# Retention's second half: output projection in three passes of rounded parts and remainders, one batch later; ScalarE takes the first ternary step

## The chip, the core and the metric

The kernel runs on one core of a Trainium2 chip. The metric is the device time of one execution in microseconds (us). TensorE (PE) multiplies, VectorE (DVE), ScalarE (ACT) and GpSimd (POOL) work on rows, and SyncE (SP) issues most DMAs. Each engine runs its own instructions in order and waits on semaphores.

## What is computed

The reference is two layers, each an attention-like block and a feed-forward block. The change lies in the first block, a retention, and in the preparation of weights for the next one:

```python
O = jnp.einsum('hst,bthe->bshe', A, V).reshape(b, s, dim)
mu = O.mean(axis=-1, keepdims=True)
var = O.var(axis=-1, keepdims=True)
Y = (O - mu) / jnp.sqrt(var + GN_EPS) * gn_gamma + gn_beta
W = jax.nn.relu(x @ wg_w)
return W * Y @ wo_w
...
def weight_quant(w):            # of w1, w3 and w2 of the feed-forward block
    scale = 1.0 / jnp.clip(jnp.mean(jnp.abs(w)), EPS)
    return jnp.clip(jnp.round(w * scale), -1.0, 1.0) / scale
```

There are 8 batches of 256 rows of 512 columns. A row block is 128 rows (a chunk), so a batch has two.

## The kernel before

`retention` has two halves. The first leaves V in `vt` (v_rows in the profile), the gate W transposed in `wt` (gate_t), and the summed scores in `at` (a_t). The second half, the one that changes, is one block of code in which the engines meet at a barrier before and after. For each batch b:

- PE: `turn` (L744) transposes the two chunks of normalised rows y; then `pv(b+1)` (L729, L732) makes the attention output of the next batch in `o_bank`; then the projection (L756) multiplies gated rows z_t by `wo` in fp32 into `p_bank`, 4 matmuls a chunk, each recorded as two.
- ACT: L776 scales and shifts the transposed rows from `y_bank` into z_t, four instructions a chunk.
- DVE: `gate` (L819) multiplies z_t by W; `normalise(b+1)` is bn_stats (L209) and its small followers (L212 to L216), POOL's power for the reciprocal root (L222), and L812, which writes y; `residual` (L823) adds `p_bank` to x.

Beside this runs the preparation of the feed-forward block. ACT sums |w3| and |w2| (`abs_sum`, L358). From batch 3 (QUIET) on, DVE turns half a weight a batch into ternary values in three steps over 2816 columns: `to_grid` (L371), `off_grid` (L377) and the cast into tern_w (L835), which counts up `tern_ready`. The first two tiles of the feed-forward's rows are normalised early too (`ffn.moments`, `ffn.normal` L288, `ffn.grid` L300, `ffn.integers` L307).

SP issues 28 DMA transposes in a fixed order, after the loads of wo and of two weights: 11 of w1 and 11 of w3 (L680), which write over v_rows that are no longer needed; two of quantised rows (L320); four of w2 (L683). `first_batch_past` is 3 for w1 and 6 for w3: so many batches' v_rows must be free. In the kernel before, a batch of v_rows is free once `pv` has read it, so SP waits for `o_ps`, the count of finished output chunks.

After the block, `bit_ffn` starts: its first matmuls (L968) need the barrier, which waits for all engines, SP among them, and the transposed rows and w1.

Of the kernel before, what the change touches and what calls it, by code (L numbers as in the profile page):

```python
# [336 lines left out]
def retention(nc, st, keep, sem, sbuf, psum, a, x, x_rows, ctx_rows, ident, powers, tern, w_mean, raw, vt, turned, kt_d, vc_d, upto):  # L337
# [311 lines left out]
    with ExitStack() as sb_:  # L649
        wo = sbuf(sb_, "wo", [P, KD, D])  # L650
        gam = sbuf(sb_, "gn_gamma", [P, KD])
        bet = sbuf(sb_, "gn_beta", [P, KD])
        y = sbuf(sb_, "gn_y", [P, CB, D])
        zt = sbuf(sb_, "z_t", [P, CB, D])
# [8 lines left out]
        o_ps, y_ready, y_ps, y_scaled, z_ready, p_ps, x_added = (  # L663
            sem(n) for n in ("o_ps", "y_ready", "y_ps", "y_scaled", "z_ready", "p_ps", "x_added"))
# [5 lines left out]
        def _(sp):  # L670
# [25 lines left out]
            sp.wait_ge(o_ps, CB * B)  # L696
# [2173 lines left out]
```

## Time and profile before

| what | us |
|---|---|
| median of 3 runs (1151.67 to 1154.88) | 1152.2 |
| the profiled execution, its own time | 1151.06 |
| its span | 1149.2 |
| PE busy in the span | 1072.1 (93%) |
| second half of retention, first matmul to last residual | 133.75 to 241.34 |
| first matmul of the feed-forward block | 242.02 |

Times in the rows are counted from the start of the span. The span leaves out 1.9 us of the execution. The blocks follow each other with barriers, and PE is busy nearly throughout, so a block that ends later moves what follows.

### The profile page before, as it was taken

Reading aid. Unit: us, or ns where it says so; the run is one execution under the profiler, and the core shown is the slowest. Engines: PE = TensorE matmul, PEld = TensorE weight load, DVE = VectorE, ACT = ScalarE, POOL = GpSimd, SP = SyncE. Lnnn points to the kernel's source line nnn. Section 1 sums busy time; section 2 is a strip of 40 time slices with the busy share of each in tenths; the row PEclk is TensorE's granted clock in tenths of the full one; section 3 lists DMA queues with packets and bytes.
Section 4 is the critical chain, followed back from the end, with each engine's and each line's share of the span. In section 5 each row is a group of like instructions: output and inputs, shape, how many; then the busy total and the mean of one; then the engine's idle time right before and its main releaser. Section 6 shows DMA issues by size and latency. Waiting matters only on the chain. (4 is left out here: it accounts for less than half of the span.)

```text
span 1149.2 us, 21701 instructions
## 1 busy us (share of the span) xinstructions
PE 1072.1 (93%) x5899; PEld 813.8 (71%) x5912; DVE 836.3 (73%) x1579; ACT 475.3 (41%) x1011; POOL 444.5 (39%) x355
## 2 busy tenths in 40 slices
PE   7999799989996998999899987999999999999997
PEld 7989765634443577888887665777777777777773
DVE  4548457969998557778897985868688687766656
ACT  2232235246562378878322162333333333333320
POOL 0000012225541101766761002666666666556620
PEclk9999999999997998999898998999999999999998
DMA  8424350433334586573264314889899899787759
GB/s 304 156 92 173 133 182 10 85 66 66 62 65 81 195 300 230 177 255 121 73 233 165 83 37 153 227 203 257 188 254 254 201 259 256 194 200 185 140 120 366
DMA packets 148189, 195.49 MB, mean 170 GB/s; under 512 B 62985, under 2 KB 80777, under 8 KB 148144
## 3 DMA queue, kind: packets, MB, share of 16 engines
q1 hardware_dynamic: 130512, 156.61, 42.8%
q0 software_dynamic: 17632, 38.32, 16.8%
q8 instruction: 23, 0.38, 0.2%
q14 instruction: 22, 0.18, 0.1%
HBM read 136.56 MB, written 50.34 MB: 163 GB/s over the span
## 5 line engine op out<-in xcount | busy, mean ns | idle before, releaser
L2462 POOL DMA_INDIRECT y_d<-tail,x_ox x78 | 144.0, 1846 | 124.3 <-ACT tail L2689 107.7
L1738 POOL DMA_INDIRECT e_rows<-r_d,x_ix x80 | 103.3, 1291 | 115.4 <-issue 96.3
L2534 PE MATMUL x_h<-x_w_hi,x_t_hi 128*128 x320 | 127.9, 400 | 2.2 <-DVE x_t_lo L2703 2.2
L2535 PE MATMUL x_h<-x_w_lo,x_t_hi 128*128 x320 | 127.7, 399 | 0.0
L2536 PE MATMUL x_h<-x_w_hi,x_t_lo 128*128 x320 | 127.6, 399 | 0.0
L2703 DVE TENSOR_TENSOR x_w_lo<-w,x_w_hi (+1 forms) x64 | 112.5, 1759 | 9.8 <-ACT x_w_hi L2660 2.6
L2651 ACT ACTIVATE e_rows<-x_h 128x256 f32<-128x256 f32 x80 | 30.8, 385 | 184.1 <-PE x_h L2536 184.1
L222 POOL TENSOR_TENSOR ln_rstd<-ln_ve,powers 128x2 f32<-128x2 f32 (+1 forms) x40 | 35.1, 878 | 165.8 <-DVE ln_ve L216 165.8
L2703 DVE TENSOR_TENSOR x_t_lo<-x_xb,x_t_hi 128x512 fp32r<-128x512 f32 x80 | 55.2, 691 | 44.6 <-ACT x_t_hi L2646 43.3
L1615 DVE SCALAR_TENSOR_TENSOR raw<-h_qk,h_d 128x768 f32<-128x768 f32 x64 | 58.2, 950 | 25.4 <-PE h_qk L1494 9.2
L2553 PE MATMUL x_o<-x_w_hi,x_avt_hi 128*128 x160 | 74.0, 463 | 1.2 <-issue 0.7
L2534 PEld LDWEIGHTS x_h<-x_w_hi,x_t_hi 128*128 128x128 f32 x320 | 60.9, 190 | 17.5 <-issue 2.6
L2535 PEld LDWEIGHTS x_h<-x_w_lo,x_t_hi 128*128 128x128 f32 x320 | 60.9, 190 | 14.9
L2536 PEld LDWEIGHTS x_h<-x_w_hi,x_t_lo 128*128 128x128 f32 x320 | 60.8, 190 | 14.9
L1381 ACT ACTIVATE h_d<-h_negm,h_g 128x256 f32<-128x256 f32 x128 | 63.7, 497 | 6.3 <-DVE h_negm L1595 2.9
L756 PE MATMUL p_bank<-wo,z_t 128*128 128x512 f32 x128 | 58.3, 610 | 6.9 <-DVE z_t L819 6.9
L2750 DVE SCALAR_TENSOR_TENSOR e_rows<-e_rows,x_rw,x_h 128x256 f32<-128x256 f32 x80 | 38.2, 477 | 35.7 <-ACT e_rows L2651 34.8
L2554 PE MATMUL x_o<-x_w_lo,x_avt_hi 128*128 x160 | 63.2, 395 | 0.0
L627 PE MATMUL ring<-xt,wg 128*128 128x256 f32 x256 | 56.6, 379 | 0.0
L1508 PE MATMUL h_pv<-h_v,raw 128*128 128x99 f32 x256 | 55.3, 300 | 0.0
L2689 ACT COPY tail<-x_o 128x512 f32<-128x512 f32 x78 | 46.0, 589 | 18.2 <-PE x_o L2559 18.2
L1509 PE MATMUL h_pv<-h_v,raw 128*128 128x99 f32 x256 | 52.9, 291 | 0.0
(419 smaller groups left out, 2564.6 us busy)
## 6 DMA issues: line engine op xcount, KB each, us to landing
w<-in_L_ffn_w SPq DMA_DIRECT2D x32, 1024.0 KB, 9.2
w<-in_L_ffn_w SPq DMA_DIRECT2D x32, 512.0 KB, 8.3
h_negm<-negm_d SPq DMA_DIRECT2D x15, 1024.0 KB, 7.5
raw<-in_L_ffn_w SPq DMA_DIRECT2D x3, 2816.0 KB, 16.5
x_res<-in_x SPq DMA_DIRECT2D x8, 512.0 KB, 4.5
ctx_in<-in_ctx SPq DMA_DIRECT2D x8, 512.0 KB, 3.4
kt_d<-ct SPq DMA_DIRECT2D x8, 512.0 KB, 3.3
vc_d<-ctx_in SPq DMA_DIRECT2D x8, 512.0 KB, 2.6
```

Of the source, the lines that this page charges most:

```text
L627: last = nc.tensor.matmul(ring[3 + n][:, j * S:(j + 1) * S], wg[:, k, m * P:(m + 1) * P], xt[:, k, :], start=k == 0, stop=k == KD - 1)
L756: last = nc.tensor.matmul(p_bank[c][:], zt[:, c, k * P:(k + 1) * P], wo[:, k, :], start=k == 0, stop=k == KD - 1)
L1381: nc.scalar.activation(dm[:, k % 2, j, 0:2, :], nm[:, u, h, 0:2, :], ACT.Exp, bias=gst[:, u, 0, h:h + 1])
L1615: nc.vector.scalar_tensor_tensor(cm[:, k % 2, heads], qk[:, heads, 0:3 * P], float(DH) ** -0.5, dm[:, k % 2, heads].rearrange("p j c n -> ...
L1738: nc.gpsimd.indirect_dma_start(out=xg[q][s], out_offset=None, in_=r_d, in_offset=bass.IndirectOffsetOnAxis(ap=ix[q][:, s:s + 1], axis=0), ...
L2462: nc.gpsimd.indirect_dma_start(out=y_d[s], out_offset=bass.IndirectOffsetOnAxis(ap=ox[q][:, s:s + 1], axis=0), in_=eo[q][s][:], in_offset= ...
L2534: nc.tensor.matmul(hbank[s], hi[:, k, :], w13p[0][:, at, k, :], start=k == 0, stop=False)
L2535: nc.tensor.matmul(hbank[s], hi[:, k, :], w13p[1][:, at, k, :], start=False, stop=False)
L2536: last = nc.tensor.matmul(hbank[s], lo[:, k, :], w13p[0][:, at, k, :], start=False, stop=k == KD - 1)
L2553: nc.tensor.matmul(obank[s], hi[:, f, :], w2p[0][:, at, f, :], start=f == 0, stop=False)
L2554: nc.tensor.matmul(obank[s], hi[:, f, :], w2p[1][:, at, f, :], start=False, stop=False)
L2703: return nc.vector.tensor_tensor(dst, src, hi.bitcast(F32), ALU.subtract)
```

## The change

The projection is split. `wo` becomes a rounded part `wo_hi` (ACT, once) and a remainder `wo_lo` (DVE, once), in fp32r. So does each gated chunk: `z_hi` (ACT, L807 of the changed kernel) and `z_lo` (DVE, `remainder`, L859). PE makes hi*hi, hi*lo and lo*hi: three matmuls where there was one fp32 matmul. y, z and z_lo now live in the rows of `vt` that `pv` has used (`slot`), and z_hi in used columns of the gate. PE projects batch b-1 behind `turn(b)` and `pv(b+1)`, so the projection comes a batch later. ACT takes over the first ternary step (`grid`), DVE keeps the other two (`level`, `ternary_piece`). ACT's and PE's loops are written out, and ACT's two sums of weights stand after batches 1 and 2. Since the used rows of `vt` now hold z until the projection has read it, SP's two waits are on `p_ps`, the count of projected chunks, in place of `o_ps`.

```diff
         raw = lent.enter_context(nc.sbuf_tensor("raw", [P, KF * D], F32, side="right"))
         with ExitStack() as st:
             tern = {n: sbuf(st, f"tern_{n}", [P, KF * D], BF16) for n in ("w1", "w3", "w2")}
+            with ExitStack() as same_place:
+                z_lo = sbuf(same_place, "z_lo", [P, NT, D], F32R)
             vt = sbuf(st, "v_rows", [P, NT, D])
             w_mean = sbuf(st, "w_mean", [P, 3])
             turned = Turned(sem, raw, vt)
...
-        wo = sbuf(sb_, "wo", [P, KD, D])
+        with ExitStack() as until_split:
+            wo = sbuf(until_split, "wo", [P, KD, D])
+        wo_lo = sbuf(sb_, "wo_lo", [P, KD, D], F32R)
+        wo_hi = sbuf(sb_, "wo_hi", [P, KD, D], F32R)
         gam = sbuf(sb_, "gn_gamma", [P, KD])
         bet = sbuf(sb_, "gn_beta", [P, KD])
-        y = sbuf(sb_, "gn_y", [P, CB, D])
-        zt = sbuf(sb_, "z_t", [P, CB, D])
...
+        def slot(b, c):
+
+            return vt[:, ds(CB * b + c, 1), :].rearrange("p o d -> p (o d)")
...
@@ -683,17 +694,16 @@
                 sp.dma_start_transpose(turned.w2t[:, :, m * P:(m + 1) * P],
                                        tern["w2"][:, m * F0:(m + 1) * F0]).then_inc(turned.w2_in, 16)
 
-            sp.wait_ge(o_ps, CB * turned.first_batch_past[0])
+            sp.wait_ge(p_ps, CB * turned.first_batch_past[0])
             for j in range(KF):
                 turn_up("w1", turned.w1t, turned.w1_in, j)
-            sp.wait_ge(o_ps, CB * turned.first_batch_past[1])
+            sp.wait_ge(p_ps, CB * turned.first_batch_past[1])
             sp.wait_ge(tern_ready, 1)
             for j in range(KF // 2):
                 turn_up("w3", turned.w3t, turned.w3_in, j)
             sp.wait_ge(tern_ready, 2)
             for j in range(KF // 2, KF):
                 turn_up("w3", turned.w3t, turned.w3_in, j)
-            sp.wait_ge(o_ps, CB * B)
             for t in range(2):
...
-            def batch(b, first=False, final=False, with_means=False):
+            def turn(b, first=False):
                 for c in range(CB):
                     pe.wait_ge(y_ready, 2 * b + c + 1)
                     if not first:
                         pe.wait_ge(y_scaled, 2 * b + c - 1)
                     for k in range(KD):
-                        last = nc.tensor.transpose(y_bank[c][:, k * P:(k + 1) * P], y[:, c, k * P:(k + 1) * P], ident[:])
+                        last = nc.tensor.transpose(y_bank[c][:, k * P:(k + 1) * P], slot(b, c)[:, k * P:(k + 1) * P], ident[:])
                     last.then_inc(y_ps, 1)
-                if not final:
-                    pv(b + 1)
-                if with_means:
-                    pe.wait_ge(abs_done, 3)
-                    nc.tensor.matmul(m_bank[:], ones[:], rsum[:, 1:3], start=True, stop=True).then_inc(mean_ps, 1)
+
+            def project(b, first=False):
                 for c in range(CB):
                     pe.wait_ge(z_ready, 2 * b + c + 1)
                     if not first:
                         pe.wait_ge(x_added, 2 * b + c - 1)
                     for k in range(KD):
-                        last = nc.tensor.matmul(p_bank[c][:], zt[:, c, k * P:(k + 1) * P], wo[:, k, :],
-                                                start=k == 0, stop=k == KD - 1)
+                        hi = z_hi[:, k, ds(S * b + c * P, P)]
+                        lo = z_lo[:, ds(CB * b + c, 1), k * P:(k + 1) * P].rearrange("p o d -> p (o d)")
+                        nc.tensor.matmul(p_bank[c][:], hi, wo_hi[:, k, :], start=k == 0, stop=False)
+                        nc.tensor.matmul(p_bank[c][:], hi, wo_lo[:, k, :], start=False, stop=False)
+                        last = nc.tensor.matmul(p_bank[c][:], lo, wo_hi[:, k, :], start=False, stop=k == KD - 1)
                     last.then_inc(p_ps, 1)
 
+            def batch(b, first=False):
+                turn(b)
+                pv(b + 1)
+                project(b - 1, first)
+
             pv(0)
-            pe.wait_ge(wo_in, 48)
-            batch(0, first=True)
-            with pe.Fori(1, QUIET) as b:
+            turn(0, first=True)
+            pv(1)
+            pe.wait_ge(wo_split, 2)
+            batch(1, first=True)
+            batch(2)
+            turn(QUIET)
+            pv(QUIET + 1)
+            pe.wait_ge(abs_done, 3)
+            nc.tensor.matmul(m_bank[:], ones[:], rsum[:, 1:3], start=True, stop=True).then_inc(mean_ps, 1)
+            project(QUIET - 1)
+            for b in range(QUIET + 1, B - 1):
                 batch(b)
-            batch(QUIET, with_means=True)
-            with pe.Fori(QUIET + 1, B - 1) as b:
-                batch(b)
-            batch(B - 1, final=True)
+            turn(B - 1)
+            project(B - 2)
+            project(B - 1)
 
...
                     last.then_inc(y_scaled, 1)
+                for c in range(CB):
+                    act.wait_ge(z_done, 2 * b + c + 1)
+                    nc.scalar.copy(z_hi[:, :, ds(S * b + c * P, P)],
+                                   slot(b, c).rearrange("p (k n) -> p k n", n=P)).then_inc(zh_ready, 1)
+
+            def grid(n):
+                (j, src), = piece_of(n)[0]
+                cols = ds(n % 2 * part, part)
+                nc.scalar.activation(src[:, cols], src[:, cols], ACT.Identity, bias=ffn.round_up[:],
+                                     scale=wrec[:, j:j + 1]).then_inc(gridded, 1)
 
             act.wait_ge(wo_in, 48)
+            nc.scalar.copy(wo_hi[:], wo[:]).then_inc(wo_split, 1)
             batch(0)
-
-            def rest(lo, hi):
-
-                with act.Fori(lo, hi) as b:
-                    act.wait_ge(p_ps, 2 * b)
-                    batch(b)
-
-            rest(1, 2)
+            batch(1)
+            abs_sum(act, 1, raw)
             act.wait_ge(ffn.round_ready, 2)
             for t in range(2):
                 ffn.normal(act, t, t)
-            rest(2, QUIET)
+            batch(2)
+            abs_sum(act, 2, raw2)
             for t in range(2):
                 ffn.grid(act, t, t)
-            abs_sum(act, 1, raw)
-            abs_sum(act, 2, raw2)
-            rest(QUIET, B)
+            batch(QUIET)
+            act.wait_ge(mean_ready, 2)
+            grid(0)
+            for b in range(QUIET + 1, B - 1):
+                batch(b)
+                grid(b - QUIET)
+            batch(B - 1)
             nc.scalar.activation(ffn.warm[:], ffn.minus[:], ACT.Silu)
 
         @block.vector
...
-                    z = zt[:, c, :].rearrange("p (k n) -> p k n", n=P)
-                    nc.vector.tensor_tensor(z, z, wt[:, :, ds(S * b + c * P, P)], ALU.mult).then_inc(z_ready, 1)
+                    dve.wait_ge(zh_ready, 2 * b + c + 1)
+                    nc.vector.tensor_tensor(z_lo[:, ds(CB * b + c, 1), :].rearrange("p o (k n) -> p (o k) n", n=P),
+                                            slot(b, c).rearrange("p (k n) -> p k n", n=P),
+                                            z_hi[:, :, ds(S * b + c * P, P)].bitcast(F32), ALU.subtract).then_inc(z_ready, 1)
 
             def residual(b, c):
                 dve.wait_ge(p_ps, 2 * b + c + 1)
                 nc.vector.tensor_tensor(x[:, ds(CB * b + c, 1), :], x[:, ds(CB * b + c, 1), :], p_bank[c][:],
                                         ALU.add).then_inc(x_added, 1)
-
-            part = KF * D // 2
...
+
             def batch(b, piece=None):
-                gate(b)
-                if piece:
-                    normalise(b + 1, between=lambda: ternary_piece(piece - 1))
-                else:
-                    normalise(b + 1)
+                gate(b, 0)
+
+                def between():
+                    gate(b, 1)
+                    if piece:
+                        level(piece - 1)
+
+                normalise(b + 1, between)
                 if piece == 0:
                     means()
-                residual(b, 0)
-                if piece is not None:
-                    if piece == 0:
-                        dve.wait_ge(mean_ready, 2)
-                    to_grid(steps, *piece_of(piece))
-                residual(b, 1)
-                if piece is not None:
-                    off_grid(steps, *piece_of(piece))
+                remainder(b)
+                if b:
+                    for c in range(CB):
+                        residual(b - 1, c)
+                if piece:
+                    ternary_piece(piece - 1)
 
             normalise(0)
+            dve.wait_ge(wo_split, 1)
+            nc.vector.tensor_tensor(wo_lo[:], wo[:], wo_hi[:].bitcast(F32), ALU.subtract).then_inc(wo_split, 1)
             batch(0)
+            batch(1)
             dve.wait_ge(x_added, CB)
             for t in range(2):
                 ffn.moments(dve, steps, t)
-            batch(1)
+            batch(2)
             for t in range(2):
                 ffn.spread(dve, steps, t, t)
             dve.wait_ge(x_added, CB + 1)
             ffn.moments(dve, steps, 2)
-            batch(2)
             for b in range(QUIET, B - 1):
                 batch(b, piece=b - QUIET)
-            gate(B - 1)
+            for c in range(CB):
+                gate(B - 1, c)
+            level(B - 2 - QUIET)
+            remainder(B - 1)
             ternary_piece(B - 2 - QUIET)
-            for c in range(CB):
-                residual(B - 1, c)
+            for b in range(B - 2, B):
+                for c in range(CB):
+                    residual(b, c)
 
     return ffn
```

In the order of instructions this shows at three places. First PE, around batch 3: the mean of the weights (m_bank) and what follows it. Before:

```order
L732 MATMUL o_bank<-v_rows,a_t 128x128
L750 MATMUL m_bank<-rsum,ones 128x2 [waits abs_done]
L756 MATMUL p_bank<-wo,z_t 128x512 [waits x_added,z_ready]
L756 MATMUL p_bank<-wo,z_t 128x512 x3
L756 MATMUL p_bank<-wo,z_t 128x512 [waits x_added,z_ready]
L756 MATMUL p_bank<-wo,z_t 128x512 x3
```

In the changed kernel, at the same place:

```order
L788 MATMUL m_bank<-rsum,ones 128x2 [waits abs_done]
L769 MATMUL p_bank<-wo_hi,z_hi 128x512 [waits x_added,z_ready]
L770 MATMUL p_bank<-wo_lo,z_hi 128x512
L771 MATMUL p_bank<-wo_hi,z_lo 128x512
L769 MATMUL p_bank<-wo_hi,z_hi 128x512
L770 MATMUL p_bank<-wo_lo,z_hi 128x512
L771 MATMUL p_bank<-wo_hi,z_lo 128x512
```

Eight matmuls became 24, and they belong to batch 2, where they belonged to batch 3.

Second DVE, in one of the later batches (4 and on), from the gate to the last ternary step. Before:

```order
L819 TENSOR_TENSOR z_t<-z_t,gate_t 128x512 [waits y_scaled] x2
L209 BN_STATS gn_st<-o_bank 128x6 [waits o_ps]
L209 BN_STATS gn_st<-o_bank 128x6
L212 COPY gn_ve<-gn_st 128x1 [waits gn_dve_step]
L214 BN_AGGR gn_mv<-gn_st 128x2 x2
L216 TENSOR_SCALAR gn_ve<-gn_mv 128x2 [waits gn_dve_step]
L835 TENSOR_SCALAR tern_w<-raw 128x2816 [waits gn_dve_step]
L812 TENSOR_SCALAR gn_y<-o_bank,gn_mv,gn_rstd 128x512 [waits gn_rstd_ready]
L812 TENSOR_SCALAR gn_y<-o_bank,gn_mv,gn_rstd 128x512
L823 TENSOR_TENSOR x_res<-x_res,p_bank 128x512 [waits p_ps]
L371 TENSOR_SCALAR raw<-raw,wrec 128x2816
L823 TENSOR_TENSOR x_res<-x_res,p_bank 128x512 [waits p_ps]
```

In the changed kernel, from the same batch's first gate:

```order
L854 TENSOR_TENSOR v_rows<-v_rows,gate_t 128x512 [waits y_scaled]
L211 BN_STATS gn_st<-o_bank 128x6 [waits o_ps]
L211 BN_STATS gn_st<-o_bank 128x6
L218 TENSOR_SCALAR gn_ve<-gn_mv 128x2 [waits gn_dve_step]
L854 TENSOR_TENSOR v_rows<-v_rows,gate_t 128x512 [waits y_scaled]
L382 TENSOR_SCALAR raw<-raw 128x2816 [waits gn_dve_step,gridded]
L848 TENSOR_SCALAR v_rows<-o_bank,gn_mv,gn_rstd 128x512 [waits gn_rstd_ready]
L848 TENSOR_SCALAR v_rows<-o_bank,gn_mv,gn_rstd 128x512
L859 TENSOR_TENSOR z_lo<-v_rows,z_hi 128x512 [waits zh_ready] x2
L865 TENSOR_TENSOR x_res<-x_res,p_bank 128x512 [waits p_ps] x2
L872 TENSOR_SCALAR tern_w<-raw 128x2816 [waits gn_dve_step]
```

Two remainders came in, one ternary step of 2816 columns went to ACT, and the second gate stands behind the statistics.

Third SP, from its first transpose to the barrier. Before:

```order
L680 DMA_TRANSPOSE v_rows<-tern_w 128x4x128 [waits o_ps]
L680 DMA_TRANSPOSE v_rows<-tern_w 128x4x128 x10
L680 DMA_TRANSPOSE v_rows<-tern_w 128x4x128 [waits tern_ready,o_ps]
L680 DMA_TRANSPOSE v_rows<-tern_w 128x4x128 x4
L680 DMA_TRANSPOSE v_rows<-tern_w 128x4x128 [waits tern_ready]
L680 DMA_TRANSPOSE v_rows<-tern_w 128x4x128 x5
L320 DMA_TRANSPOSE v_rows<-f_xq 128x4x128 [waits f_xq_ready,o_ps]
L320 DMA_TRANSPOSE v_rows<-f_xq 128x4x128 [waits f_xq_ready]
```

In the changed kernel:

```order
L691 DMA_TRANSPOSE v_rows<-tern_w 128x4x128 [waits p_ps]
L691 DMA_TRANSPOSE v_rows<-tern_w 128x4x128 x10
L691 DMA_TRANSPOSE v_rows<-tern_w 128x4x128 [waits tern_ready,p_ps]
L691 DMA_TRANSPOSE v_rows<-tern_w 128x4x128 x4
L691 DMA_TRANSPOSE v_rows<-tern_w 128x4x128 [waits tern_ready]
L691 DMA_TRANSPOSE v_rows<-tern_w 128x4x128 x5
L322 DMA_TRANSPOSE v_rows<-f_xq 128x4x128 [waits f_xq_ready] x2
L694 DMA_TRANSPOSE raw<-tern_w 128x11x128 [waits tern_ready]
L694 DMA_TRANSPOSE raw<-tern_w 128x11x128
L694 DMA_TRANSPOSE raw<-tern_w 128x11x128 [waits tern_ready]
L694 DMA_TRANSPOSE raw<-tern_w 128x11x128
L962 UNCONDITIONAL_BRANCH [waits barrier_Pool_Activation_PE_DVE_SP_release]
```

The order of SP's issues is the same; the first and the twelfth of them wait for projected chunks (6 and 12 of 16) in place of output chunks.

## Rows read from the trace of the kernel before

**Rows 1.** Timeline of PE, batches 3 to 5: start, us, engine, line, operation, [idle before].
```profile
194.04 1.04 PE L744 MATMUL y_bank<-ident,gn_y 128*128 128x128 f32 x8
...
198.49 7.03 PE L756 MATMUL p_bank<-wo,z_t 128*128 128x512 f32 x16
205.36 1.04 PE L744 MATMUL y_bank<-ident,gn_y 128*128 128x128 f32 x8
```

**Rows 2.** Timeline of DVE in batch 4.
```profile
198.69 1.30 DVE L209 BATCH_NORM_STATS2 gn_st<-o_bank 128x6 f32<-128x512 f32 x2 [0.38 <-PE o_bank L732]
...
200.44 1.62 DVE L835 TENSOR_SCALAR tern_w<-raw 128x2816 bf16<-128x2816 f32 x1
202.67 1.53 DVE L812 TENSOR_SCALAR gn_y<-o_bank,gn_mv,gn_rstd 128x512 f32<-128x512 f32 x2 [0.61 <-POOL gn_rstd L222]
204.12 0.68 DVE L823 TENSOR_TENSOR x_res<-x_res,p_bank 128x512 f32<-128x512 f32 x1
204.71 1.68 DVE L371 TENSOR_SCALAR raw<-raw,wrec 128x2816 f32<-128x2816 f32 x1
...
206.90 1.62 DVE L377 TENSOR_SCALAR raw<-raw 128x2816 f32<-128x2816 f32 x1
208.44 1.29 DVE L819 TENSOR_TENSOR z_t<-z_t,gate_t 128x512 f32<-128x512 f32 x2
```

**Rows 3.** Timeline of SP's queue: issues of transposes, merged.
```profile
159.85 14.39 SPq L680 DMA_TRANSPOSE v_rows<-tern_w  x11
...
221.95 2.50 SPq L320 DMA_TRANSPOSE v_rows<-f_xq  x2
...
224.72 3.10 SPq L683 DMA_TRANSPOSE raw<-tern_w  x2
...
233.89 2.97 SPq L683 DMA_TRANSPOSE raw<-tern_w  x2
```

**Rows 4.** Timeline of PE and of DVE at the end of the block and the start of the next.
```profile
231.78 8.83 PE L756 MATMUL p_bank<-wo,z_t 128*128 128x512 f32 x16 [2.75 <-DVE z_t L819]
...
242.02 2.32 PE L968 MATMUL g_bank<-v_rows 128*128 128x512 bf16 x11 [1.41 <-PEq L649]
...
240.65 0.69 DVE L823 TENSOR_TENSOR x_res<-x_res,p_bank 128x512 f32<-128x512 f32 x1 [2.74 <-PE p_bank L756]
```

**Rows 5.** Windows: stretch, its length, busy us (x) of each engine, PE's granted clock.
```profile
137.50:141.30 3.80, 0.09 (x2) 0.06 (x1) 2.76 (x8) 0.00 (x0) 0.69 (x1) 0.81 0.90 274
141.30:146.40 5.10, 5.10 (x24) 5.10 (x25) 1.93 (x3) 2.90 (x8) 0.00 (x0) 0.50 1.05 394
...
231.80:235.40 3.60, 3.60 (x5) 1.54 (x6) 2.06 (x2) 1.24 (x2) 0.00 (x0) 0.53 0.09 17
```

**Rows 6.** Timeline of PE in the expert block: two matmuls 24 apart.
```profile
760.86 0.39 PE L2534 MATMUL x_h<-x_w_hi,x_t_hi 128*128 x1
...
766.48 0.38 PE L2542 MATMUL x_ab<-ident,e_rows 128*128 128x128 f32 x2
```

**Rows 7.** Timeline of POOL: the power alone, and beside L835.
```profile
189.76 0.69 POOL L222 TENSOR_TENSOR gn_rstd<-gn_ve,powers 128x2 f32<-128x2 f32 x1 [11.15 <-DVE gn_ve L216]
...
200.62 2.02 POOL L222 TENSOR_TENSOR gn_rstd<-gn_ve,powers 128x2 f32<-128x2 f32 x1 [3.45 <-DVE gn_ve L216]
```

**Rows 8.** Timeline of ACT in batch 4.
```profile
194.68 2.90 ACT L776 ACTIVATE z_t<-y_bank,gn_beta,gn_gamma 128x128 f32<-128x128 f32 x8 [7.48 <-PE y_bank L744]
```

**Rows 9.** The answer on tern_w, one group: ns min/median/max, first and last start.
```profile
L358 ACT ACTIVATE tern_w<-raw x3: 4880/4881/4890, 67.8 to 179.4; 128x5632 bf16<-128x5632 f32 x3
```

**Rows 10.** Timeline of all engines, batches 0 and 1.
```profile
141.27 1.94 PE L744 MATMUL y_bank<-ident,gn_y 128*128 128x128 f32 x8 [3.71 <-DVE gn_y L812]
...
148.54 1.30 DVE L209 BATCH_NORM_STATS2 gn_st<-o_bank 128x6 f32<-128x512 f32 x2 [2.46 <-PE o_bank L732]
...
151.19 1.53 DVE L812 TENSOR_SCALAR gn_y<-o_bank,gn_mv,gn_rstd 128x512 f32<-128x512 f32 x2 [0.80 <-POOL gn_rstd L222]
...
156.14 0.69 DVE L209 BATCH_NORM_STATS2 ln_st<-x_res 128x6 f32<-128x512 f32 x1
```

**Rows 11.** Timeline of ACT: the second normalisation of early rows.
```profile
162.32 0.81 ACT L288 ACTIVATE f_xn<-x_res,f_nmr,ln_rstd 128x512 f32<-128x512 f32 x1 [2.81 <-POOL f_nmr L282]
```

More of the change, by code:

```diff
@@ L334, in spread, with retention @@
     nc.vector.reciprocal(scale[:], step).then_inc(ready, 1)
-def retention(nc, st, keep, sem, sbuf, psum, a, x, x_rows, ctx_rows, ident, powers, tern, w_mean, raw, vt, turned, kt_d, vc_d, upto):
+def retention(nc, st, keep, sem, sbuf, psum, a, x, x_rows, ctx_rows, ident, powers, tern, w_mean, raw, vt, z_lo, turned, kt_d,
+              vc_d, upto):
+    with ExitStack() as same_place:
+        z_hi = sbuf(same_place, "z_hi", [P, KD, T], F32R)
     wt = sbuf(st, "gate_t", [P, KD, T])
@@ L662, in retention @@
         wo_in, dve_step = sem("wo_in"), sem("gn_dve_step")
-        o_ps, y_ready, y_ps, y_scaled, z_ready, p_ps, x_added = (
-            sem(n) for n in ("o_ps", "y_ready", "y_ps", "y_scaled", "z_ready", "p_ps", "x_added"))
+        o_ps, y_ready, y_ps, y_scaled, z_done, zh_ready, z_ready, p_ps, x_added, wo_split, gridded = (
+            sem(n) for n in ("o_ps", "y_ready", "y_ps", "y_scaled", "z_done", "zh_ready", "z_ready", "p_ps", "x_added",
+                             "wo_split", "gridded"))
+        def slot(b, c):
+            return vt[:, ds(CB * b + c, 1), :].rearrange("p o d -> p (o d)")
         QUIET = 3
@@ L706, in _ @@
             ffn.constants(pool)
-            for b in range(2):
+            for b in range(3):
                 norm.power(pool, powers, b + 1, CB)
@@ L710, in _ @@
                 ffn.column(pool, t)
-            norm.power(pool, powers, 3, CB)
+            norm.power(pool, powers, 4, CB)
             ffn.column(pool, 2)
-            for b in range(3, QUIET + 2):
-                norm.power(pool, powers, b + 1, CB)
+            norm.power(pool, powers, QUIET + 2, CB)
             pool.wait_ge(mean_sb, 1)
@@ L723, in _, with piece_of @@
             ffn.scales(pool, 0, 0)
+        part = KF * D // 2
+        def piece_of(n):
+            return [(1, raw), (2, raw2)][n // 2:n // 2 + 1], n % 2 * part, part
         def pv(b):
@@ L775, in batch @@
                     for k in range(KD):
-                        last = nc.scalar.activation(zt[:, c, k * P:(k + 1) * P], y_bank[c][:, k * P:(k + 1) * P],
+                        last = nc.scalar.activation(slot(b, c)[:, k * P:(k + 1) * P], y_bank[c][:, k * P:(k + 1) * P],
                                                     ACT.Identity, bias=bet[:, k:k + 1], scale=gam[:, k:k + 1])
                     last.then_inc(y_scaled, 1)
+                for c in range(CB):
[7 more added lines that the diff above has]
+                                     scale=wrec[:, j:j + 1]).then_inc(gridded, 1)
             act.wait_ge(wo_in, 48)
+            nc.scalar.copy(wo_hi[:], wo[:]).then_inc(wo_split, 1)
             batch(0)
-            def rest(lo, hi):
-                with act.Fori(lo, hi) as b:
-                    act.wait_ge(p_ps, 2 * b)
-                    batch(b)
-            rest(1, 2)
+            batch(1)
+            abs_sum(act, 1, raw)
             act.wait_ge(ffn.round_ready, 2)
@@ L811, in normalise, with gate, remainder @@
                 for c in range(CB):
-                    nc.vector.tensor_scalar(y[:, c, :], o_bank[c][:], norm.mv[:, c, 0:1], norm.rstd[:, c:c + 1],
+                    nc.vector.tensor_scalar(slot(b, c), o_bank[c][:], norm.mv[:, c, 0:1], norm.rstd[:, c:c + 1],
                                             ALU.subtract, ALU.mult).then_inc(y_ready, 1)
-            def gate(b):
+            def gate(b, c):
+                dve.wait_ge(y_scaled, 2 * b + c + 1)
+                z = slot(b, c).rearrange("p (k n) -> p k n", n=P)
+                nc.vector.tensor_tensor(z, z, wt[:, :, ds(S * b + c * P, P)], ALU.mult).then_inc(z_done, 1)
+            def remainder(b):
                 for c in range(CB):
-                    dve.wait_ge(y_scaled, 2 * b + c + 1)
-                    z = zt[:, c, :].rearrange("p (k n) -> p k n", n=P)
-                    nc.vector.tensor_tensor(z, z, wt[:, :, ds(S * b + c * P, P)], ALU.mult).then_inc(z_ready, 1)
+                    dve.wait_ge(zh_ready, 2 * b + c + 1)
+                    nc.vector.tensor_tensor(z_lo[:, ds(CB * b + c, 1), :].rearrange("p o (k n) -> p (o k) n", n=P),
+                                            slot(b, c).rearrange("p (k n) -> p k n", n=P),
+                                            z_hi[:, :, ds(S * b + c * P, P)].bitcast(F32), ALU.subtract).then_inc(z_ready, 1)
             def residual(b, c):
```

9 lines of the change are left out of this document (5 added, 4 removed).

## Prediction

> **What bounds the kernel now.** I read the windows and the waits of the block first, then the timelines of its engines, then SP's own queue. From batch 3 on PE never waits: from one turn to the next it takes 11.32 us, 4.45 for the turn and the output of the next batch, 6.87 for the projection [rows 1]. The reader sees DVE almost as full: between two statistics its rows add up to 11.0 us, with 0.6 and some 0.3 idle among them [rows 2]. So a shorter projection gains little unless DVE gets shorter too. SP is not on the path: its last transposes are issued at 236.9 [rows 3], PE and DVE end at 241.34, and the next block's first matmul comes 0.7 us after that [rows 4]. That margin of 4.4 us is what I follow below. PE's clock matters too: behind 3.8 us of idle PE it ran at 0.50, the lower of its levels (1.2 GHz), for 5.1 us, and behind the idle 2.75 us at the end it did so again [rows 4, 5].
>
> **The projection.** An fp32 matmul of 512 columns takes 6.87 / 8 = 0.86 us [rows 1]. The nearest rows for the new form are the experts' matmuls on rounded parts, with the same shapes: 24 of them take 5.62 us, 0.234 each [rows 6]. A batch has 24, so 5.62 in place of 6.87: 1.25 less, and PE's batch is 10.07. If they went no faster than the fp32 halves (0.43), it would be 10.3 and the batch 14.7; nothing in the trace speaks for that.
>
> **DVE.** Its prices, start to start [rows 2]: statistics with their followers 1.75, L835 1.6, the pair that writes y 1.45, a residual 0.6, L371 1.6, L377 1.54, a gate 0.6. Two remainders are two-input instructions of a gate's size, 1.2 together. L371 goes. New batch: 1.2 + 1.75 + 1.54 + 1.45 + 1.2 + 1.2 + 1.6 = 9.95, and a wait for POOL's power. That wait was 0.6, behind a power that took 2.02 us beside L835 and takes 0.69 alone [rows 2, 7]. Now the power starts a gate (0.6 us) ahead of the long instruction, so most of it is over by then; I take 0.3. DVE's batch is then 10.3, just over PE's 10.07: the late batches are paced by DVE, and take about 1.0 less than before, not 1.25.
> The Trainium skill (SBUF — State Buffer, "Who interferes with whom") says that the engine which issues first keeps the shared port pair for its whole instruction, and that the other fully blocks. The trace agrees where L835 was first. By that rule the power would hold back the long instruction here, and DVE's batch would be 10.7, which adds 1 us over three batches.
>
> **ACT.** It scales a batch in 2.90 us [rows 8]; a ternary step of half a weight is half of 4.88, some 2.6 [rows 9], the two roundings (a quarter of that each) about 1.2. Together 6.7 of 10.3 us: hidden. The split of `wo` (2048 columns, some 1.8 us on ACT and 2.5 on DVE) lies where both are idle before 148 and costs nothing; without that cover, 4 us.
>
> **The first batches.** Call turn(b)'s start T(b). Up to pv(1) nothing moves. Its end let the statistics start at 148.54 and y at 151.19 [rows 10]. PE used that time for the first projection; now there is none to do, PE idles some 3.6 us, and T(1) is 152.1 (it was 155.2). After such an idle time I expect the lower clock [rows 5]: 5.1 us in which 2.55 of work is done. Turn, pv(2) (4.45 of work) end at 159.1, the first projection at 164.7 = T(2) (before 168.3).
> Then ACT's order counts: its 4.88 us sum of w3 comes behind batch 1 (from y(2)'s gate at 161.6, plus rounding, to 167.3), then the two normalisations. From the first `moments` to the end of the second of these took 7.0 us (156.14 to 163.13) [rows 10, 11]; the moments start at 165.5 behind the residuals, so ACT is free for batch 2 at 172.5. Half its 2.9 us, a gate, the statistics and the power (2.65 together with followers) give y(3) from 177.3, so T(3) = 178.2, with PE idle from 174.8 (before 182.5). Again I count the lower clock; pv(4) ends at 185.2.
> Behind this ACT sums w2 (177.6 to 182.7), and DVE's and ACT's early rows follow one another to 185.5 (two `spread` and two `grid`). Then 1.5 to the first scaled chunk, gate 0.6, statistics and power 2.65 with the second gate between: y(4) at 190.35, T(4) = 191.2 (before 194.0). The wait for the means holds ACT's first `grid` until 192.8, so it scales batch 4 from 195.4: gate 196.9, statistics 197.6, y(5) at 201.8, T(5) = 202.7. From here DVE's 10.3: T(6) = 213.0, T(7) = 223.2 (before 228.0). PE then has turn(7), projections 6 and 7: 12.1, plus a wait of some 1.7 for the last remainders behind DVE's queue, 237.2. DVE ends at 238.0. PE and DVE thus gain 3.3 us.
>
> **SP, the step that decides.** Its twelfth transpose waits for 12 projected chunks, batches 0 to 5. Projection 5 is the last work ahead of turn(7), so it ends at 223.2. Before, this transpose waited for a cast at 202 and no longer for v_rows. Behind it in SP's order stand 11 transposes of w3, two of rows, four of w2, and then the barrier. SP issued 11 of w1 in 14.39 us, two of rows in 2.50, two of w2 in 3.10 and in 2.97 [rows 3]: 14.4 + 2.5 + 6.1 and some 0.3 between = 23.3 us, with no wait left in it, as the last cast comes at about 233. SP finishes at 246.5, 8.5 us after DVE. The next block starts 0.7 later, at 247.2, where it was 242.02: +5.2. The eleven transposes of w1 wait for 6 projected chunks now (about 191 in place of 160) and are done by 205.5, so they don't matter.
> PE has then been idle for 10 us, where it was idle for 1.4 [rows 4]. I expect the lower clock for its first 5.1 us there, 2.5 us of work lost. The first two groups of matmuls are what the block's other engines wait for, so most passes on: +2.0, with 0 and 2.5 as bounds.
> Sum: 1151.06 + 5.2 + 2.0 = 1158.3 for the profiled execution. The median of the runs is 1.1 above that execution, so 1159.
>
> **The rivals.**
> 1. The same mechanism and more of it: the remainders wait on ACT's roundings, or PE meets more of the lower clock, and the late batches stay at 11.3. T(7) is then 3 to 4 us later, SP too: 1163. For it: DVE's and PE's batches differ by 0.2 only, and each engine waits for the other in every batch. Against: the order leaves each wait a microsecond or more. Chance 0.2.
> 2. No change that can be measured: T(1) and T(3) come without the lower clock (T(7) 1.6 earlier), DVE's batch is 10.07, and the next block's start absorbs the slow matmuls. 1151.06 + 5.2 - 2.4 + 0 = 1153.9, on the median's scale 1155. For it: the two idle times are 3.6 and 3.4 us, and another of 2.75 brought the lower clock too. Chance 0.15.
> 3. Faster: SP's queue is not the last. Then the next block starts 0.7 behind DVE's 238.0, at 238.7, a gain of 3.3, and with a quick head up to 6: 1147 to 1149. It is decided by the 17 transposes: they would have to be issued in the 14.8 us between projection 5 and DVE's end, 0.87 us each, and no row shows fewer than 1.25. Or the lower-numbered wait is met earlier than I read. Chance 0.08.
> The forecast has 0.57.
>
> **How the numbers follow.** A difference of under 0.3% (3.5 us) can't be told from no change here. The forecast's own range is 1156 to 1162. To the low side I take in half of rival 2, to the high side rival 1: 1154 to 1165; outside lie rival 3 and what I don't foresee. Faster 0.08; same 0.17 (rival 2 and the low edge of the forecast); slower 0.75.
>
> **What would show it.** Right: an idle SP queue from about 205 to 223, then transposes without a gap to 246, and the barrier's end right behind the last; PE idle for 8 to 10 us before L968's successor; 24 projection matmuls in 5.6 us; DVE's late batches 10.3. The prediction is wrong if SP's first w3 transpose comes before 215, if transposes are issued faster than 1.2 us each, or if PE's idle time at batches 1 and 3 is much longer than 3.6 us.

## The result, and the profile after

The changed kernel takes 1158.87 us (median of 7 runs, 1157.56 to 1161.36), the kernel before 1151.67 (7 runs, 1148.87 to 1154.88). The ratio is 1.0079 with a 95% interval of 1.0059 to 1.0100: slower by 0.8%, 7.2 us between the medians, and within 0.2 us of the 1159 that was forecast. The profiled execution has a span of 1159.5.

First SP's queue, merged, in the changed kernel (start, us, engine, line, operation; it answers to [rows 3]):

```profile
193.41 46.45 SPq L691 DMA_TRANSPOSE v_rows<-tern_w  x22
239.91 2.57 SPq L322 DMA_TRANSPOSE v_rows<-f_xq  x2
242.52 6.57 SPq L694 DMA_TRANSPOSE raw<-tern_w  x4
```

The first row merges all 22 transposes of w1 and w3 and hides the time in which the queue stood idle. The same view asked from 209 on alone shows the eleven of w3 by themselves:

```profile
225.08 14.78 SPq L691 DMA_TRANSPOSE v_rows<-tern_w  x11
```

Those of w1 end at 208.5, so the queue waits for 16.6 us, until projection 5 ends. The last transpose is issued at 249.1, where it was 236.9. Now the end of the block, timelines of DVE and of PE (they answer to [rows 4]):

```profile
241.26 0.69 DVE L865 TENSOR_TENSOR x_res<-x_res,p_bank 128x512 f32<-128x512 f32 x1 [2.10 <-PE p_bank L771]
...
249.93 4.68 PE L1016 MATMUL g_bank<-v_rows 128*128 128x512 bf16 x12 [8.71 <-PEq L654]
254.45 2.54 PE L1016 MATMUL u_bank<-v_rows 128*128 128x512 bf16 x12
```

DVE is done at 241.95, almost when it was before (241.34). The next block starts 7.9 us later, 0.8 behind SP's last issue (a bracket gives the idle time ahead of the row and what ended it; PEq is PE's own sequencer, which here stood at the barrier). Its first group of matmuls then takes 4.5 us up to the next, where it took 2.2. These two, 7.9 and 2.4, make up the 10.2 us between the two profiled executions.

The turns of PE, from its timeline (T(1) to T(7) in the prediction's words), with two waits in the tail:

```profile
153.93 1.33 PE L758 MATMUL y_bank<-ident,v_rows 128*128 128x128 f32 x8 [3.97 <-issue]
165.87 1.03 PE L758 MATMUL y_bank<-ident,v_rows 128*128 128x128 f32 x8
180.09 1.97 PE L758 MATMUL y_bank<-ident,v_rows 128*128 128x128 f32 x8 [4.01 <-DVE v_rows L848]
193.22 1.08 PE L758 MATMUL y_bank<-ident,v_rows 128*128 128x128 f32 x8
204.51 1.37 PE L758 MATMUL y_bank<-ident,v_rows 128*128 128x128 f32 x8 [1.06 <-DVE v_rows L848]
...
214.87 1.04 PE L758 MATMUL y_bank<-ident,v_rows 128*128 128x128 f32 x8
...
224.89 1.03 PE L758 MATMUL y_bank<-ident,v_rows 128*128 128x128 f32 x8
...
235.37 0.47 PE L769 MATMUL p_bank<-wo_hi,z_hi 128*128 128x512 f32 x1 [2.39 <-DVE x_res L865]
```

T(1) to T(7) lie 1.2 to 2.0 us behind the forecast, of which 0.6 had already come up in the first half. The granted clock in the windows (columns as in [rows 5]):

```profile
134.30:137.50 3.20, 3.18 (x17) 3.20 (x18) 0.00 (x0) 0.00 (x0) 0.12 (x2) 0.58 0.49 175
...
149.90:153.90 4.00, 0.06 (x1) 0.01 (x1) 3.25 (x9) 0.62 (x1) 1.06 (x1) 1.00 1.01 414
153.90:160.50 6.60, 6.53 (x41) 6.31 (x42) 2.54 (x5) 3.41 (x9) 0.00 (x0) 0.74 0.04 17
...
180.10:187.40 7.30, 7.30 (x40) 7.29 (x41) 5.97 (x15) 6.08 (x6) 0.09 (x1) 0.59 0.00 0
187.40:193.20 5.80, 5.80 (x28) 4.72 (x27) 4.11 (x10) 3.52 (x9) 1.87 (x4) 1.00 0.00 1
...
249.80:255.50 5.70, 5.57 (x17) 2.22 (x18) 1.99 (x7) 1.66 (x2) 1.06 (x4) 0.60 0.71 115
```

Each of the long idle times of PE (ahead of turn(1), of turn(3) and of the next block) is followed by a stretch at a mean clock of 0.59 to 0.74, a mixture of its two levels; so is the one ahead of turn(0), with 0.74. The first row is another matter. It is `pv(0)`, behind 2.5 us of idle PE, at a mean clock of 0.58. Behind the same 2.5 us, with the same work, `pv(0)` ran at the full clock in the kernel before, in e1 and in all other traces below but those of e4 and e6. So behind this idle time the clock fell in some executions and not in others. Here it cost 1.6 us up to turn(0) (9.1 us from the first matmul of `pv(0)`, 7.4 in e1). Last, DVE's and POOL's timelines in a late batch (they answer to [rows 2, 7]):

```profile
209.63 1.29 DVE L211 BATCH_NORM_STATS2 gn_st<-o_bank 128x6 f32<-128x512 f32 x2
...
211.37 0.68 DVE L854 TENSOR_TENSOR v_rows<-v_rows,gate_t 128x512 f32<-128x512 f32 x1
211.97 1.62 DVE L382 TENSOR_SCALAR raw<-raw 128x2816 f32<-128x2816 f32 x1
213.67 1.53 DVE L848 TENSOR_SCALAR v_rows<-o_bank,gn_mv,gn_rstd 128x512 f32<-128x512 f32 x2
...
219.65 1.29 DVE L211 BATCH_NORM_STATS2 gn_st<-o_bank 128x6 f32<-128x512 f32 x2
...
211.55 2.08 POOL L224 TENSOR_TENSOR gn_rstd<-gn_ve,powers 128x2 f32<-128x2 f32 x1 [5.93 <-DVE gn_ve L218]
```

From statistics to statistics DVE needs 10.02 us and waits for under 0.1 us. PE's own work fills the same 10.02 us (T(6) to T(7)), so these rows alone don't say which of the two paces the batch; e4 does.

### The profile page after: what moved, and what is told of

Read it like the earlier page. It is cut to its first block and busy times, and to the rows that moved or that the text cites. A ratio compares the mean times of both kernels' runs of the same rounds, so it can differ in the third digit from the quotient of the medians.

```text
span 1159.5 us, 21780 instructions
## 1 busy us (share of the span) xinstructions
PE 1072.8 (93%) x5975; PEld 831.8 (72%) x5976; DVE 837.4 (72%) x1592; ACT 497.3 (43%) x1032; POOL 444.4 (38%) x355
## 3 DMA queue, kind: packets, MB, share of 16 engines
q0 software_dynamic: 17632, 38.32, 16.6%
## 5 line engine op out<-in xcount | busy, mean ns | idle before, releaser
L2582 PEld LDWEIGHTS x_h<-x_w_hi,x_t_hi 128*128 128x128 f32 x320 | 60.7, 190 | 17.5 <-issue 2.6
L1556 PE MATMUL h_pv<-h_v,raw 128*128 128x99 f32 x256 | 56.7, 307 | 0.0
L1557 PE MATMUL h_pv<-h_v,raw 128*128 128x99 f32 x256 | 54.1, 296 | 0.0
L1558 PE MATMUL h_pv<-h_v,raw 128*128 128x99 f32 x256 | 53.8, 295 | 0.0
```

Of the source, the lines that this page charges most:

```text
L1556: nc.tensor.matmul(pv[:, 0, span, :], c[:, 0:P], near, start=True, stop=True)
L2582: nc.tensor.matmul(hbank[s], hi[:, k, :], w13p[0][:, at, k, :], start=k == 0, stop=False)
```

## The experiments

Theory A is that SP's queue sets the end of the block and that PE's idle time behind it costs the lower clock at the next block's start. Theory B is that the block itself became slower. The ratio given with each kernel is to the kernel before, timed beside it.

**e1_w3_over_w1.**

```diff
-        self.w1t, self.w3t = (dead[:, n * j:n * (j + 1)].rearrange("p (k f) -> p k f", k=KD) for j in range(2))
+        self.w1t, self.w3t = (v.rearrange("p (k f) -> p k f", k=KD) for v in (dead[:, 0:n], over[:]))
...
-            sp.wait_ge(p_ps, CB * turned.first_batch_past[1])
+            sp.wait_ge(turned.w1_in, 16 * KF)
...
+            sp.wait_ge(p_ps, CB * turned.first_batch_past[1])
             for t in range(2):
                 ffn.turn(sp, t, t)
```

`over` is `tern["w1"]`, which the constructor gets as one more argument.

> The changed kernel, with one thing moved: w3's transposes write over tern_w1 (read by then) instead of over v_rows, so they wait for w1's transposes to land and for the casts, and no longer for 12 projected chunks; that wait now stands ahead of the two transposes of rows. Theory A (SP's queue sets the end of the block, and PE's long idle time costs the lower clock at the next block's start): w3's first five go at about 210, the last ends at 226.5, SP is done at 238, DVE's last residual at 241.95 is last, the next block starts at 242.7 in place of 249.9 and at the full clock: 7.2 + 2.4 = 9.5 us less than the changed kernel, about 1149.5, a ratio of 0.998 to the kernel before. Theory B (the block itself got slower, and SP's queue only happens to end there, so another engine would take its place): at most 2 us less than the changed kernel, 1157 or more.

Measured: 1150.64 us (12 runs), the kernel before 1149.97 (17 runs), ratio 1.0004 (0.9987 to 1.0020). SP's and PE's timelines:

```profile
209.33 17.53 SPq L691 DMA_TRANSPOSE tern_w<-tern_w  x11
226.97 2.50 SPq L322 DMA_TRANSPOSE v_rows<-f_xq  x2
229.52 7.59 SPq L694 DMA_TRANSPOSE raw<-tern_w  x4
...
242.07 2.16 PE L1017 MATMUL g_bank<-v_rows 128*128 128x512 bf16 x10 [1.41 <-PEq L654]
```

The block's own turns are within 0.5 us of where they were in the changed kernel (T(7) 224.38). Only the transposes moved, and the whole loss is gone, with the next block at 242.07 and at the full clock. Theory B falls. The ratio came out 0.002 above what was expected, and its interval allows no gain over the kernel before to be claimed.

**e2_wait_later.** `sp.wait_ge(p_ps, CB * (turned.first_batch_past[1] + 1))`, otherwise the changed kernel.

> The changed kernel, with SP's second wait on projected chunks at 14 in place of 12 (one batch later, projection 6). Theory A: projection 6 ends 7.9 us after projection 5, nothing else fills SP's queue, so the next block starts 7.9 us later and the time is about 1167. Theory B: the queue is not what the next block waits for, so 0 to 3 us more.

Measured: 1168.89 us (4 runs), ratio 1.0162 (1.0140 to 1.0184). PE's timeline:

```profile
255.43 3.87 PE L1016 MATMUL g_bank<-v_rows 128*128 128x512 bf16 x11 [16.82 <-PEq L654]
```

T(7) is 222.34 in this run, so the next block starts 33.1 us behind it, where it was 25.0: 8.1 more, as theory A had it (7.9). The profiled executions lie 8.0 us apart. The medians lie 10.0 apart, 2 more than the queue explains; with four runs over 4 us that rest stays open.

**e3_busy_pe.**

```diff
             project(B - 1)
+            pe.wait_ge(y_scaled, 2 * B)
+            for n in range(32):
+                nc.tensor.matmul(y_bank[0][:], z_hi[:, 0, 0:P], wo_hi[:, n % KD, :], start=True, stop=True)
```

> The changed kernel, with 32 more matmuls on PE behind the last projection (fp32r, 512 columns, results unused, 0.234 us each, 7.5 us in all, so over before SP is done). Theory A: the next block starts at the same time, but its first two groups of matmuls take 2.2 and 2.4 us in place of 4.5 and 2.4: 2.4 us less, about 1156.5. Theory B (the start of the next block waits on other engines anyway): no change, 1159.

Measured: 1158.66 us (6 runs), ratio 1.0071 (1.0056 to 1.0087). The timeline:

```profile
240.31 7.50 PE L797 MATMUL y_bank<-wo_hi,z_hi 128*128 128x512 f32 x32
248.47 2.32 PE L1019 MATMUL g_bank<-v_rows 128*128 128x512 bf16 x11 [0.66 <-PEq L654]
```

The clock stayed up (first group 2.15 us to the next, at 250.62). But the filling ended at 247.8, behind SP's last issue at 246.7, and delayed the start: it came 25.8 us behind T(7), 0.8 more than in the changed kernel. So 1.6 of 2.4 us remained, and the times of whole runs can't tell that from nothing. From the first matmul of the feed-forward block to the start of its last residual it is 125.8 us in the changed kernel and 123.4 in the kernel before and in e1: the lower clock's 2.4 us pass on to the end of that block. Here it is 124.1. Up to the last residual but three e3 is 2.4 us shorter than the changed kernel too (104.8 and 107.2); the 0.7 us lost behind it have another reason, which no run looks into. So the trace shows the price of the lower clock, and the times of whole runs don't.

**e4_two_passes.** Without `nc.tensor.matmul(p_bank[c][:], hi, wo_lo[:, k, :], ...)`.

> The changed kernel without the pass of z_hi with wo_lo, so its projection is less exact: 16 matmuls a batch in place of 24, PE's batch 8.2 us in place of 10.07. Theory that DVE paces the late batches: they stay at 10.0 us, PE idles 1.8 in each, and T(7) moves by under 0.5 us for batches 4 to 6. Rival that PE paces them: they shrink to under 9.5 us, and the next block starts 2 us or more earlier.

Measured, one run: 1162.83 us; span 1161.0. Windows from turn(4) to turn(5), turn(5) to turn(6), turn(6) to turn(7):

```profile
192.85:204.43 11.58, 8.64 (x56) 7.32 (x57) 8.49 (x17) 8.47 (x12) 5.94 (x4) 1.00 0.50 99
204.43:215.95 11.52, 10.26 (x56) 8.94 (x57) 9.96 (x17) 6.65 (x12) 3.19 (x2) 0.85 0.12 24
215.95:225.97 10.02, 8.62 (x57) 7.32 (x57) 9.88 (x17) 6.67 (x12) 2.10 (x2) 1.00 0.01 2
```

DVE's timeline, ahead of the statistics that `pv(6)` releases:

```profile
211.04 1.30 DVE L211 BATCH_NORM_STATS2 gn_st<-o_bank 128x6 f32<-128x512 f32 x2 [1.42 <-PE o_bank L746]
```

A third less projection work buys nothing. The undisturbed batch takes 10.02 us, DVE's time, with PE busy for 8.6 of it: DVE paces. The batch before took 11.52: behind 2.9 us of idle PE its clock was 0.85, `pv(6)` came late, and DVE waited 1.4 us for it. T(7) came 82.65 us behind T(0), 1.1 more than in the changed kernel, where under 0.5 was expected. The next block did not start later for it (249.64, in the changed kernel 249.93), since SP's queue decides there. It is one run, so its 1162.83 us are not compared.

**e5_fp32_later.** The split undone, the rest of the change kept:

```diff
-                        nc.tensor.matmul(p_bank[c][:], hi, wo_hi[:, k, :], start=k == 0, stop=False)
-                        nc.tensor.matmul(p_bank[c][:], hi, wo_lo[:, k, :], start=False, stop=False)
-                        last = nc.tensor.matmul(p_bank[c][:], lo, wo_hi[:, k, :], start=False, stop=k == KD - 1)
+                        last = nc.tensor.matmul(p_bank[c][:], slot(b, c)[:, k * P:(k + 1) * P], wo[:, k, :],
+                                                start=k == 0, stop=k == KD - 1)
```

> The changed kernel with the split undone: one fp32 matmul of z and wo in place of the three passes, no z_hi, z_lo, wo_hi, wo_lo; a batch later, z in v_rows' place, ACT's ternary step and SP's waits stay. PE's batch is 11.31 us again, DVE's and ACT's are lighter. If the three passes gain something only where PE paces: batches 4 to 6 take 11.3 in place of 10.0 to 11.3, T(7) is 2.6 us later, SP's 25 us behind it are as long, the next block starts 2.6 us later than in the changed kernel: 1161.5, a ratio to the kernel before of 1.010. If DVE paces everything, and fewer instructions on it help: no later than the changed kernel, 1.008 or less.

Measured: 1161.55 us (6 runs, 1155.54 to 1164.13), ratio 1.0085 (1.0059 to 1.0111). The interval holds both expectations; PE's timeline decides:

```profile
201.73 1.04 PE L755 MATMUL y_bank<-ident,v_rows 128*128 128x128 f32 x8
213.04 1.04 PE L755 MATMUL y_bank<-ident,v_rows 128*128 128x128 f32 x8
224.36 1.04 PE L755 MATMUL y_bank<-ident,v_rows 128*128 128x128 f32 x8
```

The late batches take 11.31 us again, and T(7) comes 83.7 us behind turn(0) (140.65), where it was 81.5 (from 143.38). That pair flatters the passes a little: the changed kernel had spent part of its lower clock in `pv(0)`, ahead of turn(0), and e5 had not. In e1 and e3, whose `pv(0)` ran at the full clock like e5's, T(7) comes 82.2 us behind turn(0). So the three passes are worth 1.5 to 2.2 us here, less than 1.25 us for each of three late batches.

**e8_before_wait.** The kernel before, with `p_ps` in place of `o_ps` in SP's two waits.

> The kernel before, with only SP's two waits changed to projected chunks (6 and 12), as in the changed kernel. Projection 5 ends at 216.7 there, a batch ahead of the last turn but one; 23.6 us of transposes behind it end at 240.3, and DVE's last residual ends at 241.34. Theory that the wait costs only together with the batch by which the projection comes later: no change, a ratio of 1.000, with SP's queue some 1 us short of being last. Rival that the wait alone costs: the next block starts 2 us or more later, a ratio of 1.002 or more.

Measured: 1150.23 us (12 runs), ratio 1.0001 (0.9983 to 1.0018). SP's and DVE's timelines:

```profile
235.12 6.51 SPq L683 DMA_TRANSPOSE raw<-tern_w  x4
...
241.63 0.69 DVE L823 TENSOR_TENSOR x_res<-x_res,p_bank 128x512 f32<-128x512 f32 x1 [2.75 <-PE p_bank L756]
```

SP's last issue ends at 241.6, DVE's last residual at 242.3. The wait costs nothing without the batch by which the projection comes later, by a margin of 0.7 us.

**e6_rows_spread.** On top of e1; DVE's part, with ACT's and POOL's orders to match:

```diff
             dve.wait_ge(x_added, CB)
-            for t in range(2):
-                ffn.moments(dve, steps, t)
+            ffn.moments(dve, steps, 0)
             batch(2)
-            for t in range(2):
-                ffn.spread(dve, steps, t, t)
+            ffn.moments(dve, steps, 1)
+            ffn.spread(dve, steps, 0, 0)
+            batch(QUIET, piece=0)
+            ffn.spread(dve, steps, 1, 1)
...
-            for b in range(QUIET, B - 1):
+            for b in range(QUIET + 1, B - 1):
```

> The kernel with w3 over tern_w1, and the two early row tiles taken apart: the moments of the second one stand behind batch 2 on DVE, its normalisation behind batch 3 on ACT, the sum of w2 behind batch 2, the roundings of the rows behind batches 3 and 4. Theory that the 4 us in which PE idles ahead of turn(3), and the waits ahead of T(4) and T(5), come from the early rows' way DVE, POOL, ACT, DVE standing in front of batch 2: turn(3) follows at once (T(3) 175.5 in place of 179.6), the lower clock there is gone, T(7) comes at about 217 in place of 224.4, the next block 7 us earlier: 1143, a ratio of 0.993 to 0.994. Rival that ACT's sums are what fills these stretches, wherever they stand: T(7) moves by less than 3 us.

Measured: 1142.26 us (6 runs), the kernel before 1150.09 (17 runs), ratio 0.9908 (0.9884 to 0.9932). PE's timeline:

```profile
176.32 1.03 PE L758 MATMUL y_bank<-ident,v_rows 128*128 128x128 f32 x8
186.57 1.03 PE L758 MATMUL y_bank<-ident,v_rows 128*128 128x128 f32 x8
...
217.53 1.03 PE L758 MATMUL y_bank<-ident,v_rows 128*128 128x128 f32 x8
...
234.98 2.54 PE L1018 MATMUL g_bank<-v_rows 128*128 128x512 bf16 x12 [1.19 <-PEq L654]
```

PE no longer waits ahead of turn(3), and the next block starts 7.1 us earlier than in e1, as expected.

**e7_fill.** On top of e6, `fill()` ahead of turn(0) and ahead of turn(1):

```diff
+            def fill():
+                for _ in range(4):
+                    nc.tensor.matmul(fill_bank[:], at[:, 0:P], vt[:, NT - 1, :], start=True, stop=True)
```

> The kernel of the line before this one (rows taken apart), with four fp32 matmuls of 512 columns (3.4 us, results unused) on PE ahead of turn(0) and four ahead of turn(1), where it idles 3.6 and 4.0 us. Theory that the lower clock follows from PE's idle time: the granted clock stays at 1.00 in both stretches behind, pv(1) and pv(2) take 3.6 us each in place of 5 to 6, T(2) comes 4 to 4.5 us earlier against T(0): a ratio 0.003 to 0.004 below that kernel. Rival that the clock is as low with the filling: T(2) is as late or up to 1 us later.

Measured: 1138.76 us (6 runs), ratio 0.9893 (0.9870 to 0.9917), against 0.9908 for e6: the intervals overlap. Windows behind the two fillings:

```profile
140.96:146.00 5.04, 4.98 (x41) 4.68 (x42) 3.52 (x4) 3.96 (x10) 0.00 (x0) 1.00 1.06 397
...
149.87:155.00 5.13, 5.09 (x42) 4.81 (x43) 2.70 (x5) 3.41 (x9) 0.00 (x0) 1.00 0.74 303
```

In e6 the stretches of 6.5 us behind turn(0) and turn(1), in the same columns:

```profile
143.78:150.30 6.52, 6.46 (x40) 6.08 (x40) 3.46 (x3) 3.42 (x9) 0.00 (x0) 0.74 1.05 398
...
154.31:160.80 6.49, 6.44 (x41) 6.21 (x42) 2.51 (x4) 3.40 (x9) 0.00 (x0) 0.74 0.10 39
```

The clock stays at 1.00 behind the fillings, where e6 has 0.74 in both places, and turn(2) comes 19.2 us behind turn(0) in place of 22.5. Of these 3.3 us (4 to 4.5 were expected) 1.5 were lost again in the tail of this run, where the clock fell behind the wait ahead of projection 7 (2.39 us; in e6 the clock stayed at 1.00 behind the same wait of 2.36).

**e9_tail.** On top of e7, the two residuals of batch 6 ahead of the last cast:

```diff
             remainder(B - 1)
+            for c in range(CB):
+                residual(B - 2, c)
             ternary_piece(B - 2 - QUIET)
-            for b in range(B - 2, B):
-                for c in range(CB):
-                    residual(b, c)
+            for c in range(CB):
+                residual(B - 1, c)
```

> The kernel with the filling, and in DVE's tail the two residuals of batch 6 ahead of the last ternary cast instead of behind it. Theory that projection 7 waits 2.4 us for these residuals because they stand behind the cast (1.6 us): PE's wait shrinks to about 0.8, the next block starts 1.6 us earlier behind T(7), or 2.5 to 3 if the lower clock that this run of the filled kernel showed there is gone too: a ratio of 0.987 to 0.988. Rival that the wait is for the remainders of batch 7 and only written down to the residual: no change.

Measured: 1139.53 us (6 runs), ratio 0.9921 (0.9890 to 0.9951): not told apart from e7 by whole runs, and above the 0.987 to 0.988 that was expected. The first matmul of projection 7, in e9:

```profile
220.86 0.47 PE L770 MATMUL p_bank<-wo_hi,z_hi 128*128 128x512 f32 x1 [0.84 <-DVE x_res L873]
```

and in e7:

```profile
221.88 0.77 PE L770 MATMUL p_bank<-wo_hi,z_hi 128*128 128x512 f32 x1 [2.39 <-DVE x_res L873]
```

The wait shrank as expected, and from T(7) to the next block it is 16.0 us in place of 18.9. Since 1.5 of e7's 18.9 came from its lower clock there, the fair pair is with e6, 17.5: the order of the residuals is worth 1.5 us. e6, e7 and e9 beat both kernels; between the three only the traces tell.

## Why the prediction was right

**SP decides.** This was the step on which the forecast rested, and it held: 17 transposes behind projection 5, 24.2 us from 224.9 to 249.1 (23.3 forecast; the four of w2 took 6.6 rather than 6.1). e1 took the wait away by another place and the loss with it, e2 put one batch more in and lost 8.1 us. e8 adds what the prediction didn't take apart: the wait costs only because the projection also comes a batch later, so that projection 5 is the last work ahead of turn(7) instead of turn(6).

**The lower clock at the next block.** Forecast 2.0 with bounds of 0 and 2.5, measured 2.4 in the trace, behind 8.7 us of idle PE; with PE kept busy (e3) or idle for 1.4 us only (e1) it is gone.

**The projection.** 24 matmuls take 5.6 us, as taken from the experts' rows [rows 6].

**DVE** paces the late batches, at 10.02 instead of the 10.3 of the sum: the wait for the power, taken as 0.3, is under 0.1 us. The reason given for the 0.3 was wrong all the same. The power was to be mostly over before the long instruction; it takes 2.08 us as before (1.07 in batch 2, beside a gate alone), and only ends with the long instruction instead of 0.6 behind it.
By the rule of the Trainium skill (SBUF — State Buffer, "Who interferes with whom") the power, issued 0.4 us ahead of L382, would hold that one back. It didn't: L382 followed the gate at once. The gate, which reads two inputs from SBUF, was there before the power, and the rule as stated does not say that DVE's next instruction goes first again; here it did, in all three late batches, and the measurement decides.

**The first batches.** The idle times ahead of turn(1) and turn(3) were forecast at 3.6 and 3.4 us and came at 4.0 and 4.0, with the lower clock behind both. T(1) and T(3) came 1.8 and 1.9 late, for the most part for the reasons that are given for T(7) below. e6 shows that the idle time ahead of turn(3) was the way of the early rows, DVE to POOL to ACT and back; ACT's sum, which the prediction also named, wasn't last in it. (e6 moves several steps at once; the sum of w3 stays where it was.)

**What was off.** The tail: PE's wait for the last remainders was put at 1.7, and PE waited 1.2 and 2.4 us there, both for residuals; the second stood behind the last ternary cast on DVE, as e9 shows. So PE and DVE did not gain the 3.3 us that the sum had for them: DVE ended 0.6 later than before. It lay under SP's queue and cost nothing, but it is most of why e1 only draws level: there, with T(7) where the forecast had it counted from `pv(0)`, the next block comes 17.7 us behind T(7) instead of the sum's 15.5.

T(7) came 1.7 later than forecast: 0.6 from the first half, and 1.1 behind `pv(0)`, which the sum had at the full clock. From the first matmul of `pv(0)` the forecast had 89.5 us to T(7); it is 90.6 here, and 89.6 in e1 and e3, whose `pv(0)` kept the full clock. The start of the next block was forecast at 247.2 and came at 249.9: these 1.7, 0.9 for the transposes and 0.1 for the step from SP's last issue to the first matmul. With 0.4 more for the lower clock the profiled execution took 1161.3 in place of 1158.3.

**Luck.** That the median hit to 0.1 us is luck. The sum was 3.0 short for the profiled execution, and the step from there to the median, taken as +1.1 from the kernel before, was -2.4: that execution was among the slower ones of the changed kernel, whose seven times lie in two groups (three at 1161.3, four at 1157.6 to 1158.9). Why they do, no run shows.

**The rivals.** Rival 1 fell with T(5) to T(7), which lie 10.4 and 10.0 us apart. Rival 2 had DVE's batch right (10.07), but the clock fell behind T(1) and T(3), and the next block did not absorb its 2.4 us. Rival 3 fell with 17 transposes at 1.4 us each.

## What to carry to other kernels

When a buffer gets a second use, look for who waits for its release and what stands behind that waiter in its queue: here 17 issues and a barrier stood behind one wait, and another place for one result undid the loss of 0.8%. When an engine is made lighter, ask first who paces the batch: a third less projection left DVE's 10.02 us as they were. A change whose pieces shift work between engines can be judged piece by piece only with the others in place, as the wait alone and the split alone show.

## What the runs showed that was not expected

Less work on PE made a batch slower (e4, one run): with 16 matmuls a batch in place of 24, 2.9 us of idle time ahead of turn(5) were followed by a clock of 0.85 and a batch of 11.5 us instead of 10.4. And matmuls whose results nobody uses paid for themselves in the trace (e7): 8 of them, 6.9 us of PE in its idle time, brought turn(2) 3.3 us nearer to turn(0); whole runs don't tell e7 from e6. Last, the same work behind the same idle time can meet the lower clock in one execution and not in another: behind 2.5 us of idle PE `pv(0)` took 3.8 us in eight of the eleven traces and 5.4 in three.
